# Cross-attention on one core: the loads of contexts 2 to 15 move from SyncE's queue to GpSimd's, all six of a batch together

## The reference

```
q = x @ Wq + bq;  k = ctx @ Wk + bk;  v = ctx @ Wv + bv
attn = softmax(q k^T / sqrt(64))            # per head
out = (attn v) @ Wo + bo
y = layernorm(x + out) * gamma + beta
```

## Time and profile before

| | |
|---|---|
| median of 3 runs | 970.45 us (970.04 to 970.47) |
| the profiled execution | 960.75 us, its span 958.9 us |
| busy: PE, DVE, ACT, POOL | 894.0, 829.1, 742.2, 287.0 us |
| loads of contexts | 48 DMAs of whole tiles, 48 of tails, all on SP's queue |
| DMA transposes of tiles | 200 of `p_hi`, 200 of `p_lo` |
| HBM read | 15.35 MB |

### The profile page before, as it was taken

One profiled execution on the slowest core, in us unless ns is written; L12 is line 12 of the kernel. 1 busy time (PEld: TensorE's weight loads), 2 busy tenths in 40 slices (PEclk: granted clock), 3 DMA queues, 4 the chain that ended last, 5 costly groups with the idle time before them and its releaser, 6 DMA issues.

```text
span 958.9 us, 25367 instructions
## 1 busy us (share of the span) xinstructions
PE 894.0 (93%) x10366; PEld 681.1 (71%) x10366; DVE 829.1 (86%) x1071; ACT 742.2 (77%) x1083; POOL 287.0 (30%) x330
## 2 busy tenths in 40 slices
PE   8889998898999999999999999999989898899996
PEld 7567866676777777767677677767767676677775
DVE  4889879897998989899898989989889798898983
ACT  3777877787787888778788777878877787788973
POOL 3050672323232331423314133242413223133001
PEclk8989999999999999999999999999999999999998
DMA  8687998999999999999999999999999999999996
GB/s 220 140 163 160 179 189 157 188 204 189 206 193 198 201 194 207 211 192 192 190 208 180 208 190 200 206 190 192 184 204 196 184 202 154 203 192 195 208 165 126
DMA packets 683064, 181.16 MB, mean 189 GB/s; under 512 B 654596, under 2 KB 682052, under 8 KB 682948
## 3 DMA queue, kind: packets, MB, share of 16 engines
q1 hardware_dynamic: 681332, 178.48, 97.4%
q10 hardware_dynamic: 1344, 0.53, 0.2%
q0 software_dynamic: 272, 0.53, 0.2%
HBM read 15.35 MB, written 0.82 MB: 17 GB/s over the span
## 4 chain that ended last, share of the span: by engine, by line
PE 49%; DMA 19%; DVE 16%; SPq 9%; issue 5%; ACT 1%; POOL 1%; POOLq 0%; DVEq 0%; ACTq 0%
PE ps L527 21%; DMA pt_lo<-p_lo 17%; PE ps L541 11%; PE ps L546 9%; DVE nmax L748 7%; DVE p_lo L763 5%; PE ps L396 4%; SPq L328 3%; SPq L336 2%; PE ps L390 2%; SPq L284 1%; SPq L288 1%; DMA pt_hi<-p_hi 1%; DVE c_max L668 1%; POOL early_sb L997 1%
## 5 line engine op out<-in xcount | busy, mean ns | idle before, releaser
L748 DVE TENSOR_REDUCE nmax<-ps 128x1 f32<-128x1446 f32 x200 | 332.1, 1660 | 76.3 <-PE ps L527 75.4
L763 DVE SCALAR_TENSOR_TENSOR p_lo<-p,rinv,p_hi 128x1444 f16<-128x1444 f32 x200 | 370.2, 1851 | 14.4 <-DMA pt_lo<-p_lo 13.2
L866 ACT ACTIVATE p<-ps,nmax 128x1446 f32<-128x1446 f32 x200 | 292.1, 1460 | 21.9 <-DVE nmax L748 21.6
L874 ACT ACTIVATE p_hi<-p,rinv 128x1444 f16<-128x1444 f32 x200 | 298.7, 1493 | 0.2 <-DMA pt_hi<-p_hi 0.2
L541 PE MATMUL ps<-pt_hi,c_hi 128*128 128x128 f16 (+1 forms) x2288 | 269.6, 217 | 3.2 <-DMA pt_hi<-p_hi 2.7
L541 PE MATMUL ps<-pt_hi,c_lo 128*128 128x128 f16 (+1 forms) x2288 | 269.6, 217 | 0.0
L541 PEld LDWEIGHTS ps<-pt_hi,c_hi 128*128 128x128 f16 x2288 | 217.9, 98 | 28.2 <-issue 7.7
L541 PEld LDWEIGHTS ps<-pt_hi,c_lo 128*128 128x128 f16 x2288 | 217.5, 98 | 20.1 <-issue 0.5
L546 PE MATMUL ps<-pt_lo,c_hi 128*128 128x128 f16 (+1 forms) x2288 | 158.2, 218 | 48.0 <-DMA pt_lo<-p_lo 47.5
L546 PEld LDWEIGHTS ps<-pt_lo,c_hi 128*128 128x128 f16 x2288 | 130.3, 98 | 57.3 <-DMA pt_lo<-p_lo 56.7
L886 ACT ACTIVATE o_t<-ps,unscale 128x128 f32<-128x128 f32 (+1 forms) x208 | 74.5, 362 | 110.1 <-PE ps L546 109.5
(11 more groups left out here) (108 smaller groups left out, 680.7 us busy)
## 6 DMA issues: line engine op xcount, KB each, us to landing
c_raw<-in_ctx_dram SPq DMA_DIRECT2D x32, 256.0 KB
pt_hi<-p_hi SPq DMA_TRANSPOSE x200, 3.4
pt_lo<-p_lo SPq DMA_TRANSPOSE x200, 3.7
c_raw<-in_ctx_dram SPq DMA_DIRECT2D x16, 192.0 KB
c_raw<-in_ctx_dram SPq DMA_DIRECT2D x48, 18.0 KB
out_dram<-y SPq DMA_DIRECT2D x16, 50.0 KB
x_sb<-in_x_dram SPq DMA_DIRECT2D x1, 600.0 KB
o_t<-in_L_xattn_Wq_dram SPq DMA_DIRECT2D x2, 256.0 KB, 4.4
```

The lines of the kernel that those rows point to most:

```text
L748: dve.tensor_reduce(nmax[:, n % RING:n % RING + 1], ps[:, bank:bank + 3, 0:KEYW], AX.XY, ALU.max, negate=True).then_inc(s_nm, 1)
L763: dve.scalar_tensor_tensor(out=p_lo[:, par, 0:KL], in0=p32[:, n % P32S, 0:KL], scalar=rinv[:, i:i + 1], in1=p_hi[:, par, 0:KL], op0=ALU.mu ...
L866: act.activation(p32[:, n % P32S, :].rearrange("p (k w) -> p k w", w=KEYW), ps[:, bank:bank + 3, 0:KEYW], ACT.Exp, bias=nmax[:, i:i + 1], ...
L874: act.activation(p_hi[:, par, 0:KL], p32[:, n % P32S, 0:KL], ACT.Copy, scale=rinv[:, i:i + 1]).then_inc(s_hi, 1)
```

## The change

The loads of contexts 0 and 1 stay on SP's queue in the prologue. Those of contexts 2 to 15 (14 batches, six DMAs each) leave SP's loop; POOL issues all six of batch w+2 in a row at the top of its pass for window w, in front of `query_scales(w + 1)`, and waits for the same split of batch w before. That pass begins when POOL has finished the rows of batch w-2, that is, at the end of window w-1. The two queues' loads count on semaphores of their own.

```
+        def load_context(eng, b, g):
+            a, e = TG * g, min(TG * g + TG, KT - 1)
+            par = b % 2
+            whole = ctx_in[b:b + 1, a * P:e * P, :].rearrange("o (t p) d -> p (o t) d", p=P)
+            eng.dma_start(c_raw[:, par, a:e, :], whole).then_inc(s_c[min(b, 2 + par)], 16)
+            if g == NT - 1:
+                ... # the three tails, likewise
@@ SP's loop over the tiles
                 w, r = window(n)
-                if LOAD_AT <= r < LOAD_AT + NT and w + 2 < B:
-                    if r == LOAD_AT:
-                        sp.wait_ge(s_chl, w + 1)
-                    load_context(w + 2, r - LOAD_AT)
@@ DVE, context_max
-                    dve.wait_ge(s_c[b % 2], context_landed(b))
+                    dve.wait_ge(s_c[min(b, 2 + b % 2)], context_landed(b))
@@ POOL's loop over the windows
             for w in range(B):
                 b = w + 1
+                if w + 2 < B:
+                    pool.wait_ge(s_chl, w + 1)
+                    for g in range(NT):
+                        load_context(pool, w + 2, g)
                 if b < B:
                     query_scales(b)
```

More of the change, by code:

```diff
@@ L55, in cross_attention_kernel @@
     G_AT_FIRST = 4
-    LOAD_AT = 1
     STORE_AT = 2
@@ L171, in cross_attention_kernel @@
         s_x = [sem(f"x_loaded{i}") for i in range(2)]
-        s_c = [sem(f"context_loaded{i}") for i in range(2)]
+        s_c = [sem(f"{who}context_loaded{i}") for who in ("", "next_") for i in range(2)]
         s_bq = sem("bq_loaded")
@@ L264, in context_landed @@
         def context_landed(b):
-            return 16 * LOADS * (b // 2 + 1)
+            return 16 * LOADS * max(b // 2, 1)
         def emptied(eng, k):
@@ L276, in cross_attention_kernel @@
         block = es.enter_context(nc.Block())
+        def load_context(eng, b, g):
[4 more added lines that the diff above has]
+            if g == NT - 1:
+                tail = ctx_in[b:b + 1, (KT - 1) * P:KL, :].rearrange("o p d -> p o d")
+                for i in range(3):
+                    eng.dma_start(c_raw[i * KTAIL:(i + 1) * KTAIL, par, KT - 1:KT, :], tail).then_inc(s_c[min(b, 2 + par)], 16)
         @block.sync
         def _(sp):
[L280 to L288, removed]
             for half in range(2):
@@ L294, in _ @@
             for g in range(NT):
-                load_context(0, g)
+                load_context(sp, 0, g)
             sp.dma_start(x_sb[:, 0:XG, :], x[0:XG, :, :].rearrange("b q d -> q b d")).then_inc(s_x[0], 16)
@@ L300, in _ @@
             for g in range(NT):
-                load_context(1, g)
+                load_context(sp, 1, g)
             sp.dma_start(x_sb[:, XG:B, :], x[XG:B, :, :].rearrange("b q d -> q b d")).then_inc(s_x[1], 16)
```

## The result

The changed kernel takes 989.25 us (median of 4 runs, 985.2 to 994.45), the kernel before 970.25 on the same chip: ratio 1.0203, 95% interval 1.0146 to 1.0259. Forecast were 965.5 us and a range of 952.5 to 981.0: the time lies outside it, on the other side.

The account below looks back on a forecast made before the run. The prediction took the kernel to run near PE's own work, with PE's idle time to win: -16 us of waits, +11 on the DMA engines, 0 on POOL, so -5 from 970.45, near 965.5 us; range 952.5 to 981.

Parts of the forecast that it names:

- The gain: PE's waits for low transposes behind SP's loads, r = 4 to 6 of windows 2 to 13, vanish: -16 us.
- The cost on the DMA engines: POOL's load as one lump at the window's edge pushes transposes back, 0.9 us in each of twelve windows: +11 us.
- The free share of the engines: Room on the DMA engines at the window's edge, 0.8 us, taken off a batch's 2.8 us, leaving 2.0.
- PE's lead: PE runs 1.1 us ahead of DVE at the window's edge; taken off 2.0 us, leaving 0.9 a window.
- the 2.8 us of a batch: Time one batch's load takes of all 16 DMA engines, scaled from POOL's queue row: 2.8 us (2.2 to 3.5).
- POOL late: Rival, 0.10: POOL's six issues exceed 5.8 us and DVE stands at `g_raw`; at 7.0 us, 7 us in all, near 972.5.
- the lump at the edge: Rival, 0.22: backlog at r = 12 to 2, lead no help, each window pays 2.0 us: +8, 978.5; at 2.8 us +18, 988.
- The forecast's own test: The forecast is wrong if PE's total wait for low transposes (L546) does not fall by at least 2 us.
- No change: Rival, 0.15: the DMA engines bound wherever the load lies; PE's waits only move to r = 12 to 2: 970.5 us.

Follow-up runs that it names:

- e2: All six loads of a batch together from SP's queue at the window's start (r = 0), instead of POOL's as in the changed kernel: 1.0023 of the kernel before, 966.4 us.
- e5: All six loads of a batch together from SP's queue at r = 6, instead of POOL's as in the changed kernel: 0.9872 of the kernel before.
- e7: All six loads together from SP's queue, at the place where POOL issues them in the changed kernel: 1.0069 of the kernel before.
- e9: Changed kernel, same queue and first issue, but the second and third part each wait a further tile: 0.9907 of the kernel before, median 968.8 us.
- e10: Kernel before with the load's parts on SP's queue at r = 4, 5, 6 instead of 1, 2, 3: 0.9842, 952.15 against 968.83 us.
- e13: The changed kernel run once more, unaltered, on another chip: 1.016 of the kernel before, 982.4 us.
- e14: Changed kernel with the load's parts dealt out about a tile apart, run again beside e13 on one chip: 0.9963 of the kernel before, 961.69 us.
- the second trace: Profiled execution of the changed kernel on another chip, in run e13: span 980.6 us.
- m1: Transfers only, not the kernel: twelve transposes alone 24.3 and 24.1 us; beside one context's load on POOL 28.2 and 27.2, SP 27.4 and 27.6, ACT 26.0 and 26.1.
- m2: Transfers only: twelve transposes alone 24.2 and 24.1 us; beside POOL's load in one go 29.6 and 28.7, dealt out 27.8 and 27.5; SP and ACT likewise tried.

## Why the prediction was wrong, step by step

- **The gain, -16 us (12.9 to 19.4): right in its place and cause, too low in its size.** The waits at r = 4 to 6 vanished as forecast, and the tiles from r = 4 to 8 became 23.6 us shorter in windows 2 to 13; so they did, by 22.4 to 24.2, in e2, e5, e7, e9, e10, e13 and e14.
- **The cost on the DMA engines, +11 us: this step failed, in its size.** The prediction said "2.0 us of a batch must push transposes back", and "what is left is 2.0 - 1.1 = 0.9 us a window". Measured are 3.1 us of waits a window, 37.6 in all; with the clock, 48.4 us from r = 1 to 3, 4.0 a window (3.5 in the second trace). Three things were wrong in it. The free share of the engines (0.8 us) was subtracted from the load as if the load went into the gaps: it was served beside the transposes, and those of that moment landed 3.6 and 4.3 us late. PE's lead was subtracted once from the load's total, but a lead covers a small delay of each transpose and not a big one of two in a row: of the first two microseconds were covered and 1.70 waited, of the second little more than that stall was covered and 2.27 waited. And the 2.8 us of a batch were nearer the upper end of 2.2 to 3.5: q0's packets took 17.3% of 20 us around this load, 3.5 us. m1 and m2 give 3.0 to 5.4.
- **What was no term at all: the clock.** After such stalls came stretches at 1.2 GHz: +11.9 us of PE's busy time in one trace, 900.4 - 894.0 = +6.4 in the other.
- **POOL late: rightly costed at nothing.** The six issues took 2.41 + 1.61 = 4.0 us, for the 4.4 forecast; `gb_b` is ready at 265.44, and DVE's `g_raw` at 274.35 waits for PE, not for it, as it does in all eight of its waits in windows 2 to 13. Nor did the issues and DVE hold each other up: twelve low parts ran beside such issues and took 1.72 or 1.73 us as before.
- **The rival that came true** is the lump at the edge: its place (r = 12 to 2), its sign (waits over 1.3 us, transposes landing late) and its condition. Its price was put at +8, and at +18 at the full 2.8 us a window; measured are +19. That +18 lies so near is luck in part, since its loss of 33.6 us was too small (48.4 and 41.6 in the traces) and so was its gain of 16. I gave it 0.22 and cut the range at 981, because I took the room in the gaps from shares averaged over 7.5 us. The forecast's own test, PE's wait at the low parts falling by over 2 us, was met (47.5 us over the whole span before, 42.1 after): it looked at one line, and the loss went to another, L536.
- **No change**, the rival by the bytes, fell too: with the same bytes the ten other placings and the changed kernel lie between 0.984 and 1.020.

The Trainium skill's rule that I weighed ("DMA: Bandwidth & Descriptors", section "Issuing engines are not separate DMA queues": another issuing engine saves only issue time) would make e7 and after equal. They are not, 1.0069 and 1.0203. The same page of the Trainium skill, section "Queues, rings and completion order", says that each DMA engine takes turns between the queues that have work, a packet at a time. If the profile's packets are those, this case would fit: on q0 a batch is 320 packets of 2.4 KB, where the same load in SP's or ACT's queue is 1600 of 0.5 KB and the transposes' packets have some 250 B (from the profile's counts of packets in m2); a turn of POOL's queue is then, by estimate, worth some ten of the transposes', and ACT's lump delayed them less (7.0 and 7.4 us at worst in m2, POOL's 10.5 and 9.3). No run here changed the packet's size with the queue held, so that this is the reason for POOL's higher price is argued, not shown.

Open stays also what lets the clock fall: e2's trace has four such stretches in windows 2 to 13 with waits of PE of 2.4 us at most, before's, with waits of up to 2.6, none but the one at 148.5 us. The clock's share of the loss is measured, its condition is not.

## What to carry to other kernels

Here a bulk load beside a stream of small, urgent transfers cost what its worst moment cost, not what the engines' mean share left: deal it out so that each part delays a transfer by less than its reader's room, and try the places for the one where that room is largest. Before moving a load to another queue, try another place in the same one: here one number (LOAD_AT 4 for 1) gained 1.6%, where the new queue lost 2%. Where a wait is to be forecast, take the landing of the one transfer that is in flight, compare it with the time at which its reader is free, and allow for what a stalled TensorE can pay in clock afterwards.

## What the runs showed that I had not expected

- A load from a second queue can delay a transpose that is ahead of it too: in m2 one was issued at 222.34 us, POOL's load from 223.46 on, and it landed after 6.2 us instead of 4.2; the next, issued during the load, after 9.3. Of the five POOL loads in one go in m1 and m2 two did this to the transpose issued 1.1 us ahead; beside the other three it landed after 4.1 to 4.3 us. In SP's queue those ahead of the load land after 3.7 to 4.4 us as ever.
- The load costs least beside the transposes on ACT's queue (1.8 to 2.3 us for 0.78 MB in one go; on POOL's 3.0 to 5.4, on SP's 3.2 to 3.4).
- After PE stalls of 1.7 and 2.3 us close together, the granted clock stood at 0.50 for 3.41 us, and eleven matmuls took 1.36 us instead of 0.78. A stall can cost more than its own time.
